# Attention a of a hybrid block: loop of four steps written out, three small jobs moved from VectorE to ScalarE

## The chip, the cores and the metric

One core of one Trainium2 chip runs the whole kernel. The metric is the device time of one execution in microseconds; the median of three runs of the kernel before is 5300.36 us (5296.66 to 5301.02). Engines are named as the profile names them: PE is TensorE's matmuls, PEld its weight loads, DVE VectorE, ACT ScalarE, POOL GpSimd, SP SyncE; a q behind the name is the engine's sequencer, which runs waits, register operations, branches and DMA issues.

## The reference

A block of four sublayers on x of shape (32, 256, 128) in float32: attention a, a mixture of experts, attention b, the mixture of experts again, each on a layer norm of x and added to x. Only attention a is touched by the change:

```python
q, k, v = split_heads(layernorm(x) @ W_qkv.T + b_qkv)      # 16 heads of 8
scores = einsum('bhid,bhjd->bhij', q, k) * 128 ** -0.5     # 256 x 256 per head
topk_scores, indices = top_k(scores, 76)                   # int(256 * 0.3) per row
masked = full(-inf); masked[..., indices] = topk_scores
attn = softmax(masked)
x = x + (attn @ v).reshape(32, 256, 128) @ W_out.T + b_out
```

So each row of 256 scores keeps its 76 largest and loses the rest before the softmax.

## The kernel before

Attention a runs before L1109, the two expert stages and attention b after it; those are not touched. Its work is cut into 64 groups, two for each of the 32 sequences: a group is 8 heads, and a head has 256 x 256 scores, so a group is 16 tiles of 128 rows x 256 scores. Several groups are under way at once, one step apart: in step t PE computes the scores of group t+1, ACT and POOL find thresholds for group t, DVE takes the largest values of group t-1, the rest of group t-2 is judged, and groups t-3 and t-2 go through exponentials and the product with v.

Every engine runs the same list of steps. `schedule` (L423) calls `step(t, b, u)` with t the step, b the sequence and u = t mod 4, which picks the buffers: step -1, steps 0 to 3 as straight code, then an `eng.Fori` of 14 trips with four steps in each (t = 4 to 59), then steps 60 to 67 as straight code. Inside the loop the values that engines wait for are computed from the loop register. Even steps also prepare the next sequence (norm, projections of q and k), odd ones finish that (rows of q, spreads, values). The order inside a step is written out by hand for every engine, and engines meet by semaphores only.

For one group, in the order of the work:

* PE writes the scores of a head into one of three PSUM banks (L644). DVE copies them to SBUF, two tiles a head (`evac`, L950 to L964); the copy (L960) also leaves each row's maximum in `mxs`. After the eighth head L964 writes the negated maxima `nmx`, and SP waits for that (`s["nmx"]`, L540), stores them to DRAM (L544) beside copies of q and k, and reads them back turned into one row of `q4x` for each head (L551). The matching row of k is the constant 1 (`onerow`, L269 and L802), so that the matmul of L671 yields scores less their row's maximum.
* ACT counts, by three passes of Sign with a running sum (L844), how many scores of a row lie above a guess; POOL moves the guess after the first two passes (`move`, L475) and after the third makes `hi_t` and `kk` (L502, L504), for which DVE waits at L1053.
* DVE takes for every tile the 16 largest values not above `hi_t` (`largest`, L966: one pass to zt, then MAX8, MATCH_REPLACE8, MAX8), and between these, piece by piece, `picks` (L991) chooses the 76th largest into `mid` and the one after it into `nxt`, and forms `fail`, 1 for a row whose threshold isn't certain. Two reduces (L1004, L1005) do the choosing.
* PE sums `fail` over the partitions (`judged`, L663, one row of 16 numbers in PSUM bank M1). In the middle of a step DVE turns them into integers (`check_flags`, L1034), reduces them to one (L1036), and its sequencer loads that one into a register and branches (`redo`, L1083): past the repair code when it is 0, which it is in all but two steps. Only then is `s["okay"]` raised (L1038), for which POOL waits before it makes `gone` (L494), the terms that push dropped scores far down.
* PE forms the scores again, less the maximum (L671), adds `gone` (L678), ACT takes exponentials (L830), PE multiplies by v (L692), and the sums, the division (`normalise`, L1019) and the output projection follow.

For the guess of the next sequence DVE also copies the rows of k and q from PSUM to `ktok` and `qtok` (`take_k` L912, `take_qr` L916), at h == 7 of even and h == 3 of odd steps.

Of the kernel before, what the change touches and what calls it, by code (L numbers as in the profile page):

```python
# [4 lines left out]
BATCH, T, D = 32, 256, 128  # L5
P = 128
# [50 lines left out]
def build(nc, x, W_qkv, b_qkv, W_out, b_out, Wq, Wk, Wv, Wp, pos, gate_w, gate_bias,  # L57
# [7 lines left out]
    with ctx:  # L65
# [17 lines left out]
        onerow = sb("onerow", [P, 1])  # L83
# [74 lines left out]
        with nc.Block() as block:  # L158
# [65 lines left out]
            def _(dve):  # L224
# [44 lines left out]
                nc.vector.tensor_reduce(onerow[:, :], ident[:, :].rearrange("p (n w) -> p n w", w=PAD16)[:, :, HD], AX, ALU.add)  # L269
# [42 lines left out]
        def ab(name, shape, dt=f32):  # L312
# [20 lines left out]
        nmx = ab("nmx", [P, NB4, GT])  # L333
# [15 lines left out]
        mid = ab("mid", [P, NB4, GT])  # L349
        fine = ab("fine", [P, NB4, GT])  # L350
        fail = ab("fail", [P, GT])
# [9 lines left out]
                      "nmx copied turned spgate out pused pt pv on own aown pown slow oc gate pgate upper vput ini inid")  # L361
        nmx_rows = nc.dram_tensor("nmx_rows", (P, GT), f32, kind="Internal").ap()
# [58 lines left out]
        BODY = (1, BATCH // 2 - 1)  # L421

        def schedule(eng, step):  # L423

            step(-1, -1, 3)
            for u in range(4):
                step(u, 0, u)
            with eng.Fori(*BODY) as i:
                for u in range(4):
                    step(i * 4 + u, i * 2 + u // 2, u)  # L430
            for i in (BODY[1], BODY[1] + 1):
                for u in range(4):
                    if 4 * i + u <= GROUPS + 3:
                        step(4 * i + u, 2 * i + u // 2, u)

        with nc.Block() as block:
            @block.gpsimd
            def _(pool):
# [31 lines left out]
                def step(t, b, u):  # L470
# [14 lines left out]
                    def outsiders(lag, heads):  # L485
# [3 lines left out]
                        for h in heads:  # L489
                            wait(pool, s["pused"], 8 * (t - lag) + h - 3)  # L490
                            pool.sem_inc(s["pgate"], 1)
                            for i in range(HALVES):
                                c = 2 * h + i
                                last = pool.tensor_scalar(gone[:, h % 4, i, :], SS[:, (u - lag) % 4, c, :], mid[:, (u - lag) % 4, c:c + 1], 0.0,  # L494
                                                          ALU.subtract, ALU.min)
# [35 lines left out]
            def _(sp):  # L531
# [4 lines left out]
                def step(t, b, u):  # L536
# [3 lines left out]
                    wait(sp, s["nmx"], t + 1)  # L540
# [3 lines left out]
                    sp.dma_start(nmx_rows, nmx[:, u, :]).then_inc(s["copied"], 16)  # L544
# [4 lines left out]
                    rows = nmx_rows.rearrange("q (e g i) -> e g i q", e=2, i=HALVES)  # L549
# [9 lines left out]
            def _(pe):  # L559
# [98 lines left out]
                def step(t, b, u):  # L658
# [4 lines left out]
                    def judged():  # L663

                        wait(pe, s["failed"], t - 1)
                        use1(m1_before(bb, "f0" if even else "f1"))
                        nc.tensor.matmul(M1[0:1, 0:GT], ones128[:, :], fail[:, :], start=True, stop=True).then_inc(s["m1"], 1)
# [119 lines left out]
            def _(act):  # L787
# [10 lines left out]
                def take_q(m, b, par, n):  # L798
                    wait(act, s["m0"], n + 1)
                    wait(act, s["copied"], COPIED * 2 * (b - 1))  # L800
                    if m == 2:
                        last = nc.scalar.activation(k4[:, par, :, :].rearrange("p c t -> p (c t)"), M0[:, :], ACT.Identity, bias=onerow[:, 0:1])  # L802
# [13 lines left out]

                take_x(0)
                for m in range(3):
                    take_q(m, 0, 0, m + 1)
                take_qn(4)  # L820
                take_v(0, 7)
# [11 lines left out]
                def step(t, b, u):  # L833
# [18 lines left out]
                    for h in range(9):  # L852
                        if h >= 2 and h % 2 == 0:
                            late, a = PAIRS[h // 2 - 1]
                            exponentials(t - late, a)
                            exponentials(t - late, a + 1)
                        if runs(t):
# [5 lines left out]
                        if even and front:  # L863
                            if h == 2:
                                take_x(m0_before(bb, "xT"))
                            if h in (4, 5, 6):
                                take_q(h - 4, bb + 1, (par + 1) % 2, m0_before(bb, ("q0", "q1", "k")[h - 4]))
                            if h == 8:
                                take_qn(m0_before(bb, "qn"))
                        if not even and h == 4 and runs(bb, 2, BATCH):  # L870
# [13 lines left out]
            def _(dve):  # L884
# [27 lines left out]
                def take_k(n):  # L912
                    wait(dve, s["m1"], n + 1)
                    V.tensor_copy(ktok[:, :, :].rearrange("p i d -> p (i d)"), M1[:, 0:T]).then_inc(s["m1c"], 1)

                def take_qr(n):  # L916
                    wait(dve, s["m0"], n + 1)
                    V.tensor_copy(qtok[:, :, :].rearrange("p i d -> p (i d)"), M0[:, 0:T]).then_inc(s["m0c"], 1)

# [16 lines left out]
                take_k(0)  # L936
                take_qr(5)
# [4 lines left out]
                def step(t, b, u):  # L942
# [7 lines left out]
                    def evac(h):  # L950
# [11 lines left out]
                        if h == 7:  # L962
                            wait(dve, s["evac"], GT * (t + 1) + GT)
                            V.tensor_scalar(nmx[:, (u + 1) % 4, :], mxs[:, (u + 1) % 4, :], -1.0, None, ALU.mult).then_inc(s["nmx"], 1)  # L964
# [26 lines left out]
                    def picks():  # L991
# [12 lines left out]
                        mids = own.mark(V.tensor_reduce(mid[:, z2, :], pick[:, 0, :, :], AX, ALU.add))  # L1004
                        nexts = own.mark(V.tensor_reduce(nxt[:, :], pick[:, 1, :, :], AX, ALU.add))  # L1005
                        yield
                        own.need(nexts)
                        apart = own.mark(V.tensor_tensor(nxt[:, :], nxt[:, :], mid[:, z2, :], ALU.is_lt))
                        yield
                        own.need(apart)  # L1010
                        positive = own.mark(V.scalar_tensor_tensor(tmp[:, :], mid[:, z2, :], 1.0e-6, nxt[:, :], ALU.is_gt, ALU.mult))
# [5 lines left out]
                        V.tensor_scalar(fail[:, :], fine[:, z2, :], -1.0, 1.0, ALU.mult, ALU.add).then_inc(s["failed"], 1)  # L1017
# [25 lines left out]
                    for h in range(8):  # L1043
# [14 lines left out]
                        if front and even and h == 7:  # L1058
# [858 lines left out]
```

## Time and profile before

| what | value |
|---|---|
| median of three runs | 5300.36 us |
| the profiled execution | 5302.46 us |
| its span | 5300.7 us |
| PE busy in the span | 4709.3 us, 89% |
| DVE busy | 4089.0 us, 77% |
| ACT busy | 3157.1 us, 60% |
| POOL busy | 2522.7 us, 48% |
| mean granted clock of TensorE | 0.814 of 2.4 GHz |

The profile is one execution on the chip, and all the rows come from it. Busy time counts compute instructions; waits, register operations and branches are not in it. An average over the span hides that the stages differ: attention a is the part up to about 2560 us, in which DVE is the fullest engine; in the parts after it PE is. In a timeline a row begins with its start in microseconds from the span's start, then its length, engine, line, operation, output and inputs; the bracket is the time that the engine sat idle before it, and what ended that.

### The profile page before, as it was taken

The numbers are of one execution on the slowest core, as the hardware profiler recorded it, in microseconds if no ns is written. First come the engines' busy times: TensorE is split into PE (matmuls) and PEld (weight loads), VectorE is DVE, ScalarE is ACT, GpSimd is POOL, SyncE is SP. The second block draws the span as 40 slices with busy tenths as digits, with TensorE's granted clock in tenths as the row PEclk, the third lists the DMA queues.
The fourth block names the chain that finished last, engine by engine and source line by source line (L and its number), as shares of the span: only waits on it lengthen the run. The fifth ranks groups of instructions, "written<-read, shape, count | busy, mean of one in ns | idle before, by whom it ended". The sixth has DMA issues, their size and how long they took to land. (4 is left out here: it accounts for less than half of the span.)

```text
span 5300.7 us, 121671 instructions
## 1 busy us (share of the span) xinstructions
PE 4709.3 (89%) x34686; PEld 3284.1 (62%) x34686; DVE 4089.0 (77%) x14487; ACT 3157.1 (60%) x10145; POOL 2522.7 (48%) x3026
## 2 busy tenths in 40 slices
PE   4588888889878898898899999899999998999998
PEld 3344444445444454454688888766666666888887
DVE  3899999999989999999588888655555555888886
ACT  3688888888867888887222222376777775222222
POOL 1466666666656666666544444311111111444444
PEclk6566666666656666656899999999999999999999
DMA  2000000000000000000234443200000001444444
GB/s 70 10 14 10 13 10 13 10 13 10 13 10 10 13 10 13 13 10 10 49 81 84 89 84 80 53 10 10 10 10 10 11 11 36 81 80 82 89 85 96
DMA packets 358589, 188.51 MB, mean 36 GB/s; under 512 B 190691, under 2 KB 346886, under 8 KB 358150
## 3 DMA queue, kind: packets, MB, share of 16 engines
q1 hardware_dynamic: 358150, 183.55, 17.3%
q8 instruction: 167, 2.74, 0.2%
q14 instruction: 272, 2.23, 0.1%
HBM read 147.04 MB, written 11.01 MB: 30 GB/s over the span
## 5 line engine op out<-in xcount | busy, mean ns | idle before, releaser
L844 ACT ACTIVATE junk<-SS,nt 128x256 bf16<-128x256 f32 x3072 | 1516.4, 501 | 207.1 <-POOL nt L482 156.5
L494 POOL TENSOR_SCALAR gone<-SS,mid 128x256 bf16<-128x256 f32 x1024 | 1181.9, 1171 | 759.8 <-DVEq L1038 576.5
L1205 POOL TENSOR_TENSOR f_hid<-f_g_m,f_cbs 128x256 f32<-128x256 f32 x1024 | 745.7, 728 | 849.0 <-DVE f_g_m L1450 622.5
L1305 ACT ACTIVATE f_th<-bank 128x256 f32<-128x256 f32 x1088 | 418.5, 385 | 1146.0 <-PE bank L1236 1146.0
L1235 PE MATMUL bank<-f_xTf,wgT 128*128 128x256 f32 x2176 | 692.6, 400 | 52.1 <-DVE f_g_m L1450 36.4
L1851 DVE TENSOR_REDUCE nmxb<-bank 128x2 f32<-128x512 f32 x512 | 329.2, 685 | 476.1 <-PE bank L1623 476.0
L1236 PE MATMUL bank<-f_xTf,wuT 128*128 128x256 f32 x2176 | 651.8, 381 | 0.0
L644 PE MATMUL bank<-k,q 32*128 32x256 f32 x2048 | 452.7, 574 | 220.0 <-DVE SS L960 216.6
L1267 PEld LDWEIGHTS bank<-wdT,f_hid 128*128 128x128 f32 x4096 | 601.0, 191 | 68.0 <-POOL f_hid L1205 13.2
L1267 PE MATMUL bank<-wdT,f_hid 128*128 128x128 f32 x4096 | 629.7, 276 | 11.0 <-POOL f_hid L1205 10.9
L844 ACT ACTIVATION_READ_ACCUMULATOR junk<-SS,nt 128x1 f32 x3072 | 594.0, 193 | 0.0
L975 DVE SCALAR_TENSOR_TENSOR zt<-SS,hi_t 128x256 f32<-128x256 f32 x1024 | 485.5, 514 | 89.2 <-issue 47.5
L671 PE MATMUL bank<-q4x,k4x 32*128 32x256 f32 x2048 | 535.1, 596 | 8.3 <-ACT pT L830 8.3
L1442 DVE SCALAR_TENSOR_TENSOR f_g_s<-f_th,bank 128x256 f32<-128x256 f32 x1088 | 451.3, 415 | 107.1 <-ACT f_th L1305 87.5
L1450 DVE TENSOR_TENSOR f_g_m<-f_g_s,bank 128x256 f32<-128x256 f32 x1088 | 455.9, 419 | 75.2 <-DVE f_g_s L1442 3.5
L1742 ACT ACTIVATE probb<-bank,nmxb 128x256 f32<-128x256 f32 x1024 | 441.6, 496 | 78.3 <-DVE nmxb L1851 78.3
L644 PEld LDWEIGHTS bank<-k,q 32*128 32x128 f32 x2048 | 264.2, 270 | 348.1 <-DVE SS L960 280.7
L1552 POOL TENSOR_TENSOR q<-qrow,mask_h 128x1024 f32<-128x1024 f32 x64 | 137.2, 2145 | 716.9 <-DMA qrow<-q_rows 652.9
L1236 PEld LDWEIGHTS bank<-f_xTf,wuT 128*128 128x128 f32 x2176 | 416.7, 191 | 57.4
L692 PE MATMUL bank<-pT,vaug 128*32 128x256 f32 x2048 | 425.5, 559 | 0.7 <-issue 0.6
L984 DVE MATCH_REPLACE8 zt<-L,zt 128x256 f32<-128x256 f32 x1024 | 409.0, 405 | 0.0
L830 ACT ACTIVATE pT<-bank 128x512 f32<-128x512 f32 x512 | 275.0, 588 | 220.6 <-PE bank L678 220.1
(233 smaller groups left out, 8037.1 us busy)
## 6 DMA issues: line engine op xcount, KB each, us to landing
f_cbs<-f_shares SPq DMA_DIRECT2D x512, 256.0 KB, 5.8
q4x<-q SPq DMA_DIRECT2D x64, 256.0 KB, 2.4
k4x<-k SPq DMA_DIRECT2D x64, 128.0 KB, 2.1
qrow<-q_rows SPq DMA_DIRECT2D x512, 8.0 KB
q_rows<-qTb SPq DMA_DIRECT2D x32, 128.0 KB, 1.7
out_dram<-xres SPq DMA_DIRECT2D x4, 1024.0 KB, 9.3
q4x<-nmx_rows SPq DMA_DIRECT2D x128, 4.0 KB
f_shares<-f_combT SPq DMA_DIRECT2D x64, 32.0 KB, 1.4
```

Of the source, the lines that this page charges most:

```text
L494: last = pool.tensor_scalar(gone[:, h % 4, i, :], SS[:, (u - lag) % 4, c, :], mid[:, (u - lag) % 4, c:c + 1], 0.0, ALU.subtract, ALU.min)
L644: last = nc.tensor.matmul(S[h % 3][:, i * T:(i + 1) * T], q4[rows(h), par, 2 * (u % 2) + h // 4, i * P:(i + 1) * P], k4[rows(h), par, u % ...
L671: nc.tensor.matmul(PT[h % 2][:, k * T:(k + 1) * T], k4x[rows(h), v, k * P:(k + 1) * P], q4x[rows(h), v, h // 4, :], start=True, stop=False)
L844: nc.scalar.activation(junk[:, c % 2, :], SS[:, uu % 4, c, :], ACT.Sign, bias=bias(c), accum_out=acc[:, k, uu % 4, c:c + 1]).then_inc(s["s ...
L975: n = own.mark(V.scalar_tensor_tensor(zt[:, i, :], SS[:, z, c, :], hi_t[:, y, c:c + 1], SS[:, z, c, :], ALU.is_le, ALU.mult))
L1205: pool.tensor_tensor(hid[:, e % NBUF, :], g_m[:, e % NBUF, :], cbs[:, par, e, :], ALU.mult).then_inc(s["hid"], 1)
L1235: nc.tensor.matmul(g[:, 0:T], wgT[:, e, :], xTf[:, par, :], start=True, stop=True)
L1236: nc.tensor.matmul(g[:, T:2 * T], wuT[:, e, :], xTf[:, par, :], start=True, stop=True).then_inc(s["gu"], 1)
L1267: last = nc.tensor.matmul(Y[par][h][:, 0:D], src[:, h * P:(h + 1) * P], wdT[:, e, :], start=(e == 0), stop=(e == NBLK - 1))
L1442: n = own.mark(V.scalar_tensor_tensor(g_s[:, e % 3, :], th[:, e % 3, :], 1.0, g[:, 0:T], ALU.add, ALU.mult))
L1450: V.tensor_tensor(g_m[:, e % NBUF if e < EB else NBUF, :], g_s[:, e % 3, :], g[:, T:2 * T], ALU.mult).then_inc(s["gm"], 1)
L1742: last = nc.scalar.activation(probb[:, u % 4, i, :], S[u % 4][:, i * T:(i + 1) * T], ACT.Exp, bias=nmx[:, u % 4, i:i + 1], scale=1.0)
```

## The change

`schedule` calls `step` for t = -1 and then for t = 0 to 67, all as straight code, and the waits are on constants. Five more edits go with it, all in attention a:

* The maxima are not negated: L964 and `nmx` go, SP waits for the copies' own semaphore and stores `mxs`, and the constant row of k is -1 (`minusrow`) in place of 1.
* `take_k` and `take_qr` are done by ACT, with `nc.scalar.copy`, at h == 7 of even and h == 2 of odd steps.
* The two reduces of `picks` are one reduce that writes both results to `mid`, which has two rows for each buffer.
* `fail` has 17 columns; the last is the sum over the 16, made by the accumulator of the same instruction, and PE sums all 17 over the partitions.
* ACT copies the 17 sums to the integers `flags`, at h == 4 after its exponentials. DVE's cast and its reduce to one number go; DVE waits for ACT's copy, raises the gate semaphore and loads the number.

```diff
@@ -266,7 +266,8 @@
                 nc.vector.tensor_copy(pext[:, mid + 2 * REL:], pext[:, mid + 2 * REL - 1:mid + 2 * REL].to_broadcast([HD, tail])).then_inc(s_pext, 1)
                 dve.wait_ge(s_const, 1)
                 nc.vector.tensor_tensor(mask_h8[:, :], mask_h16[:, 0:HG], mask_h16[:, HG:H], ALU.add)
-                nc.vector.tensor_reduce(onerow[:, :], ident[:, :].rearrange("p (n w) -> p n w", w=PAD16)[:, :, HD], AX, ALU.add)
+                own.link(nc.vector.tensor_reduce(minusrow[:, :], ident[:, :].rearrange("p (n w) -> p n w", w=PAD16)[:, :, HD], AX, ALU.add))
+                nc.vector.tensor_scalar(minusrow[:, :], minusrow[:, :], -1.0, None, ALU.mult)
                 dve.wait_ge(s_trc, (NJ + 3) // 4)
 
         def norm_dve(dve, own, b, s):
@@ -418,20 +418,12 @@
         PAIRS = ((3, 2), (3, 4), (3, 6), (2, 0))
         SUMS = ((3, 0), (3, 2), (3, 4), (3, 6))
 
-        BODY = (1, BATCH // 2 - 1)
 
         def schedule(eng, step):
 
             step(-1, -1, 3)
-            for u in range(4):
-                step(u, 0, u)
-            with eng.Fori(*BODY) as i:
-                for u in range(4):
-                    step(i * 4 + u, i * 2 + u // 2, u)
-            for i in (BODY[1], BODY[1] + 1):
-                for u in range(4):
-                    if 4 * i + u <= GROUPS + 3:
-                        step(4 * i + u, 2 * i + u // 2, u)
+            for t in range(GROUPS + 4):
+                step(t, t // 2, t % 4)
 
         with nc.Block() as block:
             @block.gpsimd
@@ -537,16 +529,16 @@
                     par = u // 2 % 2
                     if not runs(t):
                         return
-                    wait(sp, s["nmx"], t + 1)
+                    wait(sp, s["evac"], GT * t + GT)
                     sp.sem_inc(s["spgate"], 1)
                     wait(sp, s["pused"], 8 * (t - 3))
                     sp.sem_inc(s["spgate"], 1)
-                    sp.dma_start(nmx_rows, nmx[:, u, :]).then_inc(s["copied"], 16)
+                    sp.dma_start(max_rows, mxs[:, u, :]).then_inc(s["copied"], 16)
                     sp.dma_start(q4x[:, u, :, :], q4[:, par, 2 * (u % 2):2 * (u % 2) + 2, :]).then_inc(s["copied"], 16)
                     sp.dma_start(k4x[:, u, :], k4[:, par, u % 2, :]).then_inc(s["copied"], 16)
                     wait(sp, s["copied"], COPIED * (t + 1))
                     sp.sem_inc(s["spgate"], 1)
-                    rows = nmx_rows.rearrange("q (e g i) -> e g i q", e=2, i=HALVES)
+                    rows = max_rows.rearrange("q (e g i) -> e g i q", e=2, i=HALVES)
                     for e in range(2):
                         sp.dma_start(q4x[HD + PAD16 * e:P:PAD32, u, e, :].rearrange("g (i q) -> g i q", i=HALVES), rows[e],
                                      allow_slow_non_contiguous=True).then_inc(s["turned"], 16)
@@ -664,7 +656,7 @@
 
                         wait(pe, s["failed"], t - 1)
                         use1(m1_before(bb, "f0" if even else "f1"))
-                        nc.tensor.matmul(M1[0:1, 0:GT], ones128[:, :], fail[:, :], start=True, stop=True).then_inc(s["m1"], 1)
+                        nc.tensor.matmul(M1[0:1, 0:GT + 1], ones128[:, :], fail[:, :], start=True, stop=True).then_inc(s["m1"], 1)
 
                     def below_max(v, h, k):
 
@@ -814,10 +806,20 @@
                     wait(act, s["m0"], n + 1)
                     nc.scalar.activation(qnat[:, :], M0[:, 0:T], ACT.Identity, bias=bnat[:, 0:1]).then_inc(s["m0c"], 1)
 
+                def take_k(n):
+                    wait(act, s["m1"], n + 1)
+                    nc.scalar.copy(ktok[:, :, :].rearrange("p i d -> p (i d)"), M1[:, 0:T]).then_inc(s["m1c"], 1)
+
+                def take_qr(n):
+                    wait(act, s["m0"], n + 1)
+                    nc.scalar.copy(qtok[:, :, :].rearrange("p i d -> p (i d)"), M0[:, 0:T]).then_inc(s["m0c"], 1)
+
                 take_x(0)
                 for m in range(3):
                     take_q(m, 0, 0, m + 1)
                 take_qn(4)
+                take_k(0)
+                take_qr(5)
                 take_v(0, 7)
                 own.end()
 
@@ -854,6 +856,10 @@
                             late, a = PAIRS[h // 2 - 1]
                             exponentials(t - late, a)
                             exponentials(t - late, a + 1)
+                        if h == 4 and runs(t, 2):
+                            f1 = m1_before(bb, "f0" if even else "f1")
+                            wait(act, s["m1"], f1 + 1)
+                            nc.scalar.copy(flags[:, :], M1[0:1, 0:GT + 1]).then_inc(s["m1c"], 1)
                         if runs(t):
                             k, j = h // 3, h % 3
                             ready, done, bias = PASS[k]
@@ -865,8 +871,12 @@
                                 take_x(m0_before(bb, "xT"))
                             if h in (4, 5, 6):
                                 take_q(h - 4, bb + 1, (par + 1) % 2, m0_before(bb, ("q0", "q1", "k")[h - 4]))
+                            if h == 7:
+                                take_k(m1_before(bb, "ktok"))
                             if h == 8:
                                 take_qn(m0_before(bb, "qn"))
+                        if not even and front and h == 2:
+                            take_qr(m0_before(bb, "qtok"))
                         if not even and h == 4 and runs(bb, 2, BATCH):
                             wait(act, s["m0"], m0_before(bb, "oT") + 1)
                             nc.scalar.copy(oT[:, :], M0[:, 0:T]).then_inc(s["m0c"], 1)
@@ -909,14 +919,6 @@
                         n = V.tensor_scalar(xn[:, h, :], xrow(b, h), mv[:, h, 0:1], rstd[:, h:h + 1], ALU.subtract, ALU.mult)
                     n.then_inc(s["xn"], 1)
 
-                def take_k(n):
-                    wait(dve, s["m1"], n + 1)
-                    V.tensor_copy(ktok[:, :, :].rearrange("p i d -> p (i d)"), M1[:, 0:T]).then_inc(s["m1c"], 1)
-
-                def take_qr(n):
-                    wait(dve, s["m0"], n + 1)
-                    V.tensor_copy(qtok[:, :, :].rearrange("p i d -> p (i d)"), M0[:, 0:T]).then_inc(s["m0c"], 1)
-
                 def take_g(n):
                     wait(dve, s["m1"], n + 1)
                     V.tensor_tensor(gram[:, :], M1[:, 0:P], mask_bd[:, :, :].rearrange("p h d -> p (h d)"), ALU.mult).then_inc(s["m1c"], 1)
@@ -933,8 +935,6 @@
 
                 statistics(0)
                 normed(0)
-                take_k(0)
-                take_qr(5)
                 take_g(1)
                 take_mom(0, 6, 6)
                 own.end()
@@ -959,9 +959,6 @@
                             c = 2 * h + i
                             V.tensor_scalar(SS[:, (u + 1) % 4, c, :], S[h % 3][:, i * T:(i + 1) * T], 1.0, -3.0e38, ALU.mult, ALU.max,
                                             accum_out=mxs[:, (u + 1) % 4, c:c + 1]).then_inc(s["evac"], 1)
-                        if h == 7:
-                            wait(dve, s["evac"], GT * (t + 1) + GT)
-                            V.tensor_scalar(nmx[:, (u + 1) % 4, :], mxs[:, (u + 1) % 4, :], -1.0, None, ALU.mult).then_inc(s["nmx"], 1)
 
                     def largest(lag, p, between):
 
@@ -1001,20 +998,20 @@
                         above = own.mark(V.tensor_tensor(fine[:, z2, :], L[:, y, :, 0], hi_t[:, y, :], ALU.is_lt))
                         yield
                         own.need(second)
-                        mids = own.mark(V.tensor_reduce(mid[:, z2, :], pick[:, 0, :, :], AX, ALU.add))
-                        nexts = own.mark(V.tensor_reduce(nxt[:, :], pick[:, 1, :, :], AX, ALU.add))
+                        both = own.mark(V.tensor_reduce(mid[:, z2, :, :].rearrange("p a t -> p (a t)"),
+                                                        pick[:, :, :, :].rearrange("p a t j -> p (a t) j"), AX, ALU.add))
                         yield
-                        own.need(nexts)
-                        apart = own.mark(V.tensor_tensor(nxt[:, :], nxt[:, :], mid[:, z2, :], ALU.is_lt))
+                        own.need(both)
+                        apart = own.mark(V.tensor_tensor(nxt[:, :], mid[:, z2, 1, :], mid[:, z2, 0, :], ALU.is_lt))
                         yield
                         own.need(apart)
-                        positive = own.mark(V.scalar_tensor_tensor(tmp[:, :], mid[:, z2, :], 1.0e-6, nxt[:, :], ALU.is_gt, ALU.mult))
+                        positive = own.mark(V.scalar_tensor_tensor(tmp[:, :], mid[:, z2, 0, :], 1.0e-6, nxt[:, :], ALU.is_gt, ALU.mult))
                         yield
                         own.need(positive)
                         both = own.mark(V.tensor_tensor(fine[:, z2, :], fine[:, z2, :], tmp[:, :], ALU.mult))
                         yield
                         own.need(both)
-                        V.tensor_scalar(fail[:, :], fine[:, z2, :], -1.0, 1.0, ALU.mult, ALU.add).then_inc(s["failed"], 1)
+                        V.tensor_scalar(fail[:, 0:GT], fine[:, z2, :], 0.0, 0.0, ALU.is_equal, ALU.add, accum_out=fail[:, GT:GT + 1]).then_inc(s["failed"], 1)
 
                     def normalise():
 
@@ -1030,10 +1027,8 @@
 
                     def check_flags():
                         n1 = m1_before(bb, "f0" if even else "f1")
-                        wait(dve, s["m1"], n1 + 1)
-                        V.tensor_copy(flags[:, 0:GT], M1[0:1, 0:GT]).then_inc(s["m1c"], 1)
                         wait(dve, s["m1c"], n1 + 1)
-                        own.link(V.tensor_reduce(flags[:, GT:GT + 1], flags[:, 0:GT], AX, ALU.max))
+                        dve.sem_inc(s["gate"], 1)
                         redo(dve, V, z2)
                         dve.sem_inc(s["okay"], 1)
 
@@ -1055,13 +1050,9 @@
                             normalise()
                         if h == 4 and runs(t, 2):
                             check_flags()
-                        if front and even and h == 7:
-                            take_k(m1_before(bb, "ktok"))
                         if front and not even:
                             if h == 1:
                                 take_g(m1_before(bb, "gram"))
-                            if h == 3:
-                                take_qr(m0_before(bb, "qtok"))
                             if h == 5:
                                 take_mom(bb + 1, m0_before(bb, "mom"), m0_before(bb, "qtok") + 1)
                         if h == 7 and not even and tail:
...
```

## Rows read from the trace of the kernel before

**Rows 1.** Windows, 402 to 1451 us: time, then busy (count) of PE, PEld, DVE, ACT, POOL, clock, DMA.
```profile
402.00:1451.00 1049.00, 927.19 (x4538) 514.21 (x4540) 971.41 (x3782) 857.71 (x3126) 684.22 (x763) 0.64 0.07 12
```

**Rows 2.** Waits of DVE, 60 to 2560 us: line, releaser, total us, times, longest.
```profile
DVE stats L895 <- issue: 51.1, 13, 4.1
DVE zt L975 <- issue: 47.5, 34, 3.1
DVE work L1095 <- issue: 36.1, 2, 19.3
DVE zt L975 <- DVE flags L1036: 28.9, 29, 1.0
...
DVE flags L1034 <- PE bank L667: 3.8, 9, 2.3
```

**Rows 3.** Timeline of DVE, end of the even step t = 24.
```profile
1029.71 0.07 DVE L960 DVE_READ_ACCUMULATOR SS<-bank 128x1 f32 x1
1029.82 0.17 DVE L964 TENSOR_SCALAR nmx<-mxs 128x16 f32<-128x16 f32 x1
1029.92 0.42 DVE L914 COPY ktok<-bank 128x256 f32<-128x256 f32 x1
1030.26 1.11 DVE L975 SCALAR_TENSOR_TENSOR zt<-SS,hi_t 128x256 f32<-128x256 f32 x2
```

**Rows 4.** Timeline of DVE, after the flags in two straight steps past the loop.
```profile
2384.20 1.10 DVE L975 SCALAR_TENSOR_TENSOR zt<-SS,hi_t 128x256 f32<-128x256 f32 x2 [1.31 <-issue]
...
2419.03 1.10 DVE L975 SCALAR_TENSOR_TENSOR zt<-SS,hi_t 128x256 f32<-128x256 f32 x2 [0.99 <-DVE flags L1036]
```

**Rows 5.** Timeline of DVE around the flags, an even and an odd step.
```profile
1017.23 0.16 DVE L1034 CAST flags<-bank 1x16 int32<-1x16 f32 x1
...
1018.58 1.10 DVE L975 SCALAR_TENSOR_TENSOR zt<-SS,hi_t 128x256 f32<-128x256 f32 x2 [1.00 <-DVE flags L1036]
...
1051.91 0.16 DVE L1034 CAST flags<-bank 1x16 int32<-1x16 f32 x1
...
1053.56 1.10 DVE L975 SCALAR_TENSOR_TENSOR zt<-SS,hi_t 128x256 f32<-128x256 f32 x2 [1.30 <-issue]
```

**Rows 6.** Timeline of DVE, the two reduces.
```profile
1003.92 0.40 DVE L1004 TENSOR_REDUCE mid<-pick 128x16 f32<-128x240 f32 x1
1004.24 0.39 DVE L1005 TENSOR_REDUCE nxt<-pick 128x16 f32<-128x240 f32 x1
```

**Rows 7.** Costliest groups of the page, a wider reduce: busy, mean ns, idle before.
```profile
L1851 DVE TENSOR_REDUCE nmxb<-bank 128x2 f32<-128x512 f32 x512 | 329.2, 685 | 476.1 <-PE bank L1623 476.0
```

**Rows 8.** Timeline of PE, flags of an even step, then part of the odd one.
```profile
1014.82 0.21 PE L667 MATMUL bank<-fail,ones 128*1 128x16 f32 x2
...
1043.80 2.08 PE L644 MATMUL bank<-k,q 32*128 32x256 f32 x8 [0.18 <-DVE SS L960]
...
1051.36 0.21 PE L667 MATMUL bank<-fail,ones 128*1 128x16 f32 x2
1052.04 1.22 PE L644 MATMUL bank<-k,q 32*128 32x256 f32 x4 [0.47 <-DVE SS L960]
```

**Rows 9.** Groups of ACT by line, 402 to 1451 us, small copies: busy, mean ns.
```profile
L872 ACT COPY oT<-bank 128x256 f32<-128x256 f32 x14 | 5.0, 357 | 0.0
L795 ACT ACTIVATE xsum<-xsum 128x1 f32<-128x1 f32 x14 | 2.8, 203 | 0.4
```

**Rows 10.** Timeline of ACT, exponentials of the odd step.
```profile
1048.86 1.09 ACT L830 ACTIVATE pT<-bank 128x512 f32<-128x512 f32 x2 [1.54 <-PE bank L678]
...
1058.55 1.09 ACT L830 ACTIVATE pT<-bank 128x512 f32<-128x512 f32 x2 [2.95 <-PE bank L678]
```

**Rows 11.** Timeline of DVE, start of the even step t = 26.
```profile
1070.38 0.42 DVE L960 TENSOR_SCALAR_CACHE_REDUCE SS<-bank 128x256 f32<-128x256 f32 x1 [0.23 <-PE bank L644]
...
1076.99 0.88 DVE L975 SCALAR_TENSOR_TENSOR zt<-SS,hi_t 128x256 f32<-128x256 f32 x2
```

**Rows 12.** Timeline of POOL, start of the even step t = 26.
```profile
1076.59 0.20 POOL L504 TENSOR_SCALAR kk<-acc 128x16 f32<-128x16 f32 x1
```

More of the change, by code:

```diff
@@ L82, in build @@
         bqs = sb("bqs", [P, 2, 2])
-        onerow = sb("onerow", [P, 1])
+        minusrow = sb("minusrow", [P, 1])
         wvT = sb("wvT", [P, D])
@@ L332, in build @@
         mxs = ab("mxs", [P, NB4, GT])
-        nmx = ab("nmx", [P, NB4, GT])
         acc = ab("acc", [P, 3, NB4, GT])
@@ L348, in build @@
         nxt = ab("nxt", [P, GT])
-        mid = ab("mid", [P, NB4, GT])
+        mid = ab("mid", [P, NB4, 2, GT])
         fine = ab("fine", [P, NB4, GT])
-        fail = ab("fail", [P, GT])
+        fail = ab("fail", [P, GT + 1])
         flags = ab("flags", [1, GT + 1], mybir.dt.int32)
@@ L360, in build @@
         s = sems("a", "mv rstd xn m0 m0c m1 m1c var sig scores evac signs u0 u1 u2 thr failed flag okay "
-                      "nmx copied turned spgate out pused pt pv on own aown pown slow oc gate pgate upper vput ini inid")
-        nmx_rows = nc.dram_tensor("nmx_rows", (P, GT), f32, kind="Internal").ap()
+                      "copied turned spgate out pused pt pv on own aown pown slow oc gate pgate upper vput ini inid")
+        max_rows = nc.dram_tensor("max_rows", (P, GT), f32, kind="Internal").ap()
         COPIED, TURNED = 48, 32
@@ L493, in outsiders @@
                                 c = 2 * h + i
-                                last = pool.tensor_scalar(gone[:, h % 4, i, :], SS[:, (u - lag) % 4, c, :], mid[:, (u - lag) % 4, c:c + 1], 0.0,
+                                last = pool.tensor_scalar(gone[:, h % 4, i, :], SS[:, (u - lag) % 4, c, :], mid[:, (u - lag) % 4, 0, c:c + 1], 0.0,
                                                           ALU.subtract, ALU.min)
@@ L801, in take_q @@
                     if m == 2:
-                        last = nc.scalar.activation(k4[:, par, :, :].rearrange("p c t -> p (c t)"), M0[:, :], ACT.Identity, bias=onerow[:, 0:1])
+                        last = nc.scalar.activation(k4[:, par, :, :].rearrange("p c t -> p (c t)"), M0[:, :], ACT.Identity, bias=minusrow[:, 0:1])
                     else:
@@ L1086, in redo @@
                     slow = Own(dve, s["slow"])
-                    any_failed = dve.value_load(flags[0:1, GT:GT + 1], min_val=0, max_val=P)
+                    any_failed = dve.value_load(flags[0:1, GT:GT + 1], min_val=0, max_val=P * GT)
                     with dve.If(any_failed > 0):
@@ L1102, in redo @@
                                 slow.link(V.tensor_tensor(src, src, w, ALU.add))
-                                low = mid[:, z, bass.ds(c, 1)]
+                                low = mid[:, z, 0, bass.ds(c, 1)]
                                 slow.link(V.tensor_scalar(low, low, 0.0, -0.5 * FAR, ALU.mult, ALU.add))
```

## The prediction

> **What bounds the kernel now.** I read the busy time by windows first, then DVE's waits, then the timelines of one loop trip on each engine. Only the stage of attention a changes, some 2500 of the 5300.7 us. In its middle [rows 1] DVE is busy 971 of 1049 us, PE 927, ACT 858, POOL 684, and PE's granted clock averages 0.64 (mostly 1.2 GHz, the rest 2.4 GHz). Three engines are near full, so the order of the waits decides. DVE's waits over the whole stage [rows 2] are nearly all its own: 51.1 us in front of L895, 13 times, which is the jump back of the loop (14 trips, 13 jumps); 47.5 + 28.9 us in front of L975, mostly the fetch of the flags; 36.1 us in the repair path, taken in two steps. For the flags it waits on PE 9 times and 3.8 us. So DVE sets the pace, and each microsecond taken off it shortens a step until another engine is late. From start to start of L964 [one of them in rows 3] an ordinary step takes 36.2 to 36.4 us, one with a jump back 40.2, four of them 148.5.
>
> **The change part by part, on DVE's path.** There are 64 steps, 32 pairs of an even and an odd one.
>
> *Loop written out.* The jump costs 51.1 / 13 = 3.9 us [rows 2]; step against step it is 40.2 - 36.4 = 3.8. Thirteen of them: -50. PE, ACT, POOL and SP jump too, beside it. What may come in its place is the fetching of long straight code. The last steps of the kernel before are straight code already, and the two stops there that hold a skip over the repair code last 1.31 and 0.99 us [rows 4], as inside the loop: 1.30 and 1.00 [rows 5]. I cost the fetch at 0; its other end is a rival below.
> The Trainium skill (Runtime: NRT & Kernel Launch, section Instruction fetch mechanics) says that a taken branch whose target isn't in the small window of code already fetched stalls until it is. By that rule the jump of 3.9 us goes, which the sum has already; a skip that leaves the window would cost as much, which none of these rows shows.
>
> *Maxima not negated.* The last accumulator read starts at 1029.71, ktok's copy at 1029.92 [rows 3]: L964 costs 0.21 us, x 64 = -13. The sign moves into a constant row of k. SP stores mxs where it stored nmx, the same DMAs and bytes, 0.2 us earlier.
>
> *Rows copied by ScalarE.* ktok's copy holds DVE from 1029.92 to 1030.26 [rows 3] = 0.34 us, and qtok's, of the same shape, as long. Each is in 31 pairs: -21.
>
> *Two reduces made one, an accumulator added.* Now 0.32 us from start to start and 0.39 for the second = 0.71 [rows 6]. A reduce over 512 elements takes 0.685 [rows 7], and 480 some 0.64 to 0.69: -0.02 to -0.07 a step. The fail instruction gets an accumulator read, 0 to +0.08 by those in [rows 3]. Together -4 to +4 us; I take -2.
>
> *Flags fetched by ScalarE.* In an even step the cast starts at 1017.23 and work resumes at 1018.58 [rows 5]: 1.35 us. Cast and reduce are 0.39 of it; in the other 0.96 DVE's sequencer loads the flag into a register, checks it, skips the repair code and raises a semaphore, with DVE empty. Afterwards cast and reduce are gone: -0.39 at least. The load then waits for ACT's copy and no longer for DVE's own reduce, so it can run ahead beside the two score copies in front (0.7 us). No row shows a register load beside a busy DVE: this part is worth 0 to 0.7. I take the nearest cover, less some 0.15 for the order of issue: 0.39 + 0.55 = 0.9 us for an even step. Over all 64 steps -25 to -58.
> That needs the flags early. In the even step PE sums them at 1014.82, 2.4 us before the cast [rows 8, 5]. In the odd step L667 starts at 1051.36 and ends 0.3 us before the cast of 1051.91 [rows 8, 5], and in about half of the odd steps the cast follows it at once (9 of these show as waits [rows 2]). There ACT's copy (0.20 us for 128x1 to 0.36 for 128x256 [rows 9]) takes the cast's place, the register load follows it, and nothing is gained.
>
> Sum if nothing else were late: 50 + 13 + 21 + 2 + 58 = 144 us.
>
> **What is late next.**
> (a) *PE in the odd steps.* From the scores at 1043.80 PE works without a break to the flags at 1051.36 and waited only 0.18 and 0.47 us for DVE [rows 8]; at 1070.38 DVE itself waits 0.23 us for PE [rows 11]. So between 1043.8 and 1070.4 DVE can gain some 0.47 us at 1.2 GHz, where the edits save 0.34 + 0.9 + 0.21 = 1.45. That holds for about half of the 32 odd steps (in the others PE had 2.4 GHz for a while and was 1 to 2 us ahead): 16 x 1.0 = +16.
> (b) *POOL after an odd step.* It works without a break from DVE's release to 1076.59 + 0.20 [rows 12], and DVE, which needs its result, goes on at 1076.99 [rows 11]. DVE can be there 0.1 us earlier, of 0.28 saved on the way: about +4.
> (c) *PE before the first score copy of an odd step.* By my reading of those copies against L644 it has 0.3 to 0.7 us of room in a quarter of the cases and about 2 in the rest, against 1.5 saved: 8 x 1.0 = +8.
> (d) *The jump.* Its 3.8 us gave PE and POOL time to catch up; half a microsecond of each comes back: 13 x 0.3 = +4.
> Together +32, so **-112 us**, 1 us a step beside the jumps.
>
> *ACT* gets (0.36 + 0.36) / 2 + 0.2 = 0.56 us a step. It is busy 858 / 1049 = 82% of a mean step of 37.1 us [rows 1], 30.3, then 30.9 of 35.4, 87%. In odd steps it will stand behind L667: its exponentials of 1048.86 end at 1049.95 and L667 at 1051.57, 1.6 us. But it stands 2.95 us before those of 1058.55 [rows 10], which hides both. Cost 0; without that cover 1.6 + 0.56 in an odd step. The prologue, the last steps (which wait on PE) and the two repairs stay.
>
> **The time.** The sum is made against the profiled execution, 5302.46 us, and gives 5190; the median of the runs is 2.1 below it: 5188. Some of what a denser PE wins back by its clock is likelier than nothing, 2 us of term (a): I forecast **5186 us**.
>
> **Rivals.**
> 1. *The sequencer gains nothing, or ACT is in the way* (chance 0.14). If the register load still finds DVE empty, 0.5 x 32 = 16 us go; if ACT's stand behind L667 delays its sums, another 0.6 x 32 = 19: 5186 + 16 to 35 = 5202 to 5221. For it: no row of a load beside work. Against: the idle 2.95 us of ACT.
> 2. *The straight code brings waits of its own* (0.05). The loop goes, but a third of the 64 skips leave the fetched code. The longest stop in front of L975 is 3.1 us [rows 2] against 1.3: 20 x 1.8 = +36, and with like stops on ACT or PE about 50: 5236. Against: [rows 4].
> 3. *Slower* (0.04). The same at every skip and at the jump's price: 64 x 3.9 = 250 us against 112, 5300 + 138 = 5438; it is slower as soon as 29 of the 64 skips leave the fetched code. For it: each trip pays such a jump now. Against: none of the skips in the straight steps does. It is the skill's rule above turned against this change.
> 4. *PE follows* (0.09). A denser PE is granted 2.4 GHz more often, term (a) goes, and in odd steps the flags are early: 5186 - 16 - 14 = 5156, and 5300 - 144 - 5 = 5151 at most.
>
> **How the numbers follow.** The forecast has 0.67 (its own range 5168 to 5205), the rivals what stands with them, and 0.01 is left for an effect within 0.2% (10.6 us, about what a measurement of this kernel can tell from none). The range goes down to rival 4 and up past rival 1: 5150 to 5224. Faster 0.95, same 0.01, slower 0.04.
>
> **What would show it.** DVE has no wait of 3.9 us in front of L895; after the fetch of the flags it stops 0.4 to 0.5 us in even steps and about 1 us in odd ones, released by PE's L667 or ACT's copy. Four steps take 139 to 143 us. PE's waits for L960 shrink to some 0.1 us in odd steps, and DVE waits for L644 in more places than now. ACT waits 1 to 2 us for L667 in odd steps and less before L830. The forecast is wrong if four steps take over 145 us, if stops of 3 us or more stand behind the skips, or if DVE waits for ACT's work rather than PE's or POOL's.

## The result and the profile after

The changed kernel takes 5290.01 us (median of 13 runs, 5268.32 to 5301.59) against 5301.02 for the kernel before: ratio 0.9975, 95% interval 0.9964 to 0.9986. It is 11 us faster where 115 were forecast. The forecast sign was right, the size wrong by a factor of ten, and the time lies outside the range of 5150 to 5224. The profiled execution is the slowest of the 13, 5301.59 us, so its profile shows a kernel as long as the one before. One execution of the kernel before took 15943 us and one of the first experiment 8362 us; the ratios leave both out.

The middle of the stage, columns as in [rows 1]:

```profile
402.00:1451.00 1049.00, 928.03 (x4546) 510.97 (x4543) 951.35 (x3674) 866.81 (x3191) 692.32 (x765) 0.64 0.07 12
```

DVE is relieved, 951 us against 971, and PE is as busy as before, 928 us against 927, at the same granted clock of 0.64. The waits of DVE over 60 to 2560 us, which answer to [rows 2]:

```profile
DVE SS L960 <- PE bank L636: 134.3, 58, 8.3
DVE zt L972 <- issue: 62.6, 59, 3.1
DVE work L1086 <- issue: 38.4, 2, 19.6
```

The jumps' 51.1 us are gone, the stops behind the flags take 62.6 us where they took 76.4, and all of it has come back as waits for the first scores of a step (L636), 134.3 us where the whole stage had 26.5. Measured from the last L960 of a step to that of the next, averaged over t = 7 to 37, a step took 40.2, 36.3, 36.3, 36.0 us in a trip of the loop (148.8) and takes 37.1, 37.1, 37.2, 37.2 now (148.5). So what the jump took in one step is now lost in small parts in all four. What PE waits for, 330 to 1480 us (31 steps), the kernel before and then the changed one:

```profile
PE bank L644 <- DVE SS L960: 96.8, 62, 6.2
PE bank L575 <- DVE xn L909: 28.3, 16, 5.3
PE bank L702 <- DVE gram L922: 8.6, 5, 2.1
PE bank L583 <- ACT q L805: 4.6, 8, 0.8
PE bank L619 <- ACT oT L872: 0.2, 1, 0.2
```

```profile
PE bank L636 <- DVE SS L960: 31.8, 19, 3.0
PE bank L694 <- DVE gram L924: 26.0, 15, 1.9
PE bank L575 <- ACT q L797: 22.9, 16, 1.6
PE bank L611 <- ACT oT L882: 22.6, 15, 2.3
PE bank L567 <- DVE xn L919: 19.6, 16, 5.2
```

The two lines of the first list that name ACT are 4.8 us together, and 45.5 in the second: 16 times 1.4 us in even steps for the copy of q, 15 times 1.5 in odd ones for that of oT. PE also waits 26.0 us for DVE's `gram` where it waited 8.6, but it does so in the fastest kernel of all too (25.7). Here is where the waits for ACT come from, first PE, then ACT, in one odd step:

```profile
1044.89 0.22 PE L659 MATMUL bank<-fail,ones 128*1 128x17 f32 x2
1045.20 2.07 PE L636 MATMUL bank<-k,q 32*128 32x256 f32 x8
1048.66 1.20 PE L611 MATMUL bank<-gram,qnat 128*128 128x128 f32 x4 [1.38 <-ACT oT L882]
```

```profile
1045.14 0.16 ACT L862 CAST flags<-bank 1x17 int32<-1x17 f32 x1 [1.24 <-PE bank L659]
1045.21 0.50 ACT L846 ACTIVATE junk<-SS,nt 128x256 bf16<-128x256 f32 x1
...
1048.17 0.34 ACT L882 COPY oT<-bank 128x256 f32<-128x256 f32 x1
```

ACT stands (sits idle in a wait) 1.24 us before the flags, then counts six tiles, and only then copies oT, which PE's spreads (L611) wait for. In the kernel before no such stand was there, and the copy of oT was over at 1053.14, 0.9 us before PE came to its spreads (L619):

```profile
1052.78 0.36 ACT L872 COPY oT<-bank 128x256 f32<-128x256 f32 x1
...
1054.04 1.22 PE L619 MATMUL bank<-gram,qnat 128*128 128x128 f32 x4
```

In an even step it is the same with q, and here the record of PE's sum of the flags misleads:

```profile
1081.36 0.64 PE L684 MATMUL bank<-pT,vaug 128*32 128x256 f32 x2
1081.38 0.21 PE L659 MATMUL bank<-fail,ones 128*1 128x17 f32 x2
1081.78 1.49 PE L684 MATMUL bank<-pT,vaug 128*32 128x256 f32 x6
1083.21 1.50 PE L575 MATMUL bank<-xT,wqsT 128*128 128x256 f32 x4
...
1087.25 1.96 PE L575 MATMUL bank<-xT,wqsT 128*128 128x256 f32 x4 [1.48 <-ACT q L797]
```

```profile
1083.37 0.16 ACT L862 CAST flags<-bank 1x17 int32<-1x17 f32 x1 [1.03 <-remote]
```

The sum is recorded at 1081.38, but ACT gets its flags at 1083.37, just after the matmuls of the weighing (L684, the product with v), issued ahead of the sum, have ended at 1083.27. The semaphore that the sum raises tells the same in the trace: it rises at 1083.35, 1.75 us after the record has ended, and as the profile finds no record that ended then, it calls the releaser `remote`. The kernel before has the same distance of 1.75 us in 30 of its 32 even steps. In all odd steps but one, where two transposes (L701, L709 before) stand between the weighing and the sum, it is 0.01. Both ends of the ring of waits then show on DVE. The register load did run ahead in even steps: it is recorded from 1083.66 to 1083.97, while DVE copies scores until 1084.08, and DVE stops 0.51 us where [rows 5] had 1.00 behind the cast and reduce. And a step's first score copy waits 2.30 us for PE.

```profile
1064.96 0.43 DVE L960 TENSOR_SCALAR_CACHE_REDUCE SS<-bank 128x256 f32<-128x256 f32 x1 [2.30 <-PE bank L636]
...
1084.60 1.10 DVE L972 SCALAR_TENSOR_TENSOR zt<-SS,hi_t 128x256 f32<-128x256 f32 x2 [0.51 <-issue]
```

### The profile page after: what moved, and what is told of

It reads as the page before. It is cut to its first block and busy times, and to the rows that moved or that the text cites. A ratio compares the mean times of both kernels' runs of the same rounds, so it can differ in the third digit from the quotient of the medians.

```text
span 5299.8 us, 115583 instructions
## 1 busy us (share of the span) xinstructions
PE 4712.4 (89%) x34686; PEld 3276.2 (62%) x34686; DVE 4037.9 (76%) x14232; ACT 3170.0 (60%) x10273; POOL 2533.6 (48%) x3026
## 5 line engine op out<-in xcount | busy, mean ns | idle before, releaser
L486 POOL TENSOR_SCALAR gone<-SS,mid 128x256 bf16<-128x256 f32 x1024 | 1204.0, 1191 | 645.4 <-DVEq L1033 465.8
L972 DVE SCALAR_TENSOR_TENSOR zt<-SS,hi_t 128x256 f32<-128x256 f32 x1024 | 484.5, 514 | 85.7 <-issue 62.6
L636 PE MATMUL bank<-k,q 32*128 32x256 f32 x2048 | 430.6, 555 | 104.5 <-DVE SS L960 99.6
L960 DVE TENSOR_SCALAR_CACHE_REDUCE SS<-bank 128x256 f32<-128x256 f32 x1024 | 385.0, 413 | 134.3 <-PE bank L636 134.3
L684 PE MATMUL bank<-pT,vaug 128*32 128x256 f32 x2048 | 429.8, 565 | 10.9 <-issue 10.8
L1226 PEld LDWEIGHTS bank<-f_xTf,wgT 128*128 128x128 f32 x2176 | 331.5, 192 | 119.5 <-DVE f_g_m L1441 107.4
```

Of the source, the lines that this page charges most:

```text
L636: last = nc.tensor.matmul(S[h % 3][:, i * T:(i + 1) * T], q4[rows(h), par, 2 * (u % 2) + h // 4, i * P:(i + 1) * P], k4[rows(h), par, u % ...
L972: n = own.mark(V.scalar_tensor_tensor(zt[:, i, :], SS[:, z, c, :], hi_t[:, y, c:c + 1], SS[:, z, c, :], ALU.is_le, ALU.mult))
L1226: nc.tensor.matmul(g[:, 0:T], wgT[:, e, :], xTf[:, par, :], start=True, stop=True)
```

## The experiments

Theory A1: ACT's stand before the flags delays its copies of q and oT, and a ring of waits runs through these, PE's next scores and DVE's first score copy. Theory A2: PE's own work at the granted clock is a floor of 148 us for four steps. Times of four steps are measured as above. Each result is a median; the ratio is to the kernel before on the same chip, with its 95% interval.

**Loop written out, nothing else.**

```diff
-            with eng.Fori(*BODY) as i:
...
+            for t in range(GROUPS + 4):
+                step(t, t // 2, t % 4)
```

> The kernel before with the loop written out and nothing else. Theory A (a ring of waits through PE is nearly as tight as DVE's own pace, and the 3.9 us pause at each jump was time in which PE and POOL caught up): most of the 50 us of jumps is given back as waits of DVE for the first scores of a step, 5 to 25 us faster than before. Theory B (the jumps are a plain loss of DVE, and the loss sits in the other edits): 40 to 50 us faster than before, about 5255.

5254.57 us, ratio 0.9907 (0.9892 to 0.9922). Theory B was right on this term: 47 us, the jumps' -50 of the sum. Four steps take 144.8 us, and apart from two stops of 3.1 us behind the repairs, which the kernel before has too, DVE's longest stop behind a skip is 1.34 us (1.33 before). PE's work is the same here, at a granted clock of 0.65, so A2's floor of 148 us isn't one.

**The changed kernel with the loop kept.**

```diff
-            for t in range(GROUPS + 4):
-                step(t, t // 2, t % 4)
+            with eng.Fori(*BODY) as i:
...
```

> The changed kernel with the loop of four steps put back, all other edits kept. Theory A: DVE has slack in every step now, so the jumps fall into it: within 15 us of the changed kernel, about 5290 to 5305. Theory B: the jumps cost 50 us again: 5340.

5267.29 us, 0.9932 (0.9919 to 0.9946): faster than the changed kernel by 23 us. Neither theory had that. Writing out the loop is worth 47 us alone and does harm beside the late flags. With the loop the step with the jump takes 38.5 us and the three behind it 37.0, 35.7 and 35.2 instead of 37.1 to 37.2. PE's waits for q fall from 22.9 to 12.3 us, those for oT only from 22.6 to 20.2.

**Flags copied by DVE again, the other edits kept.**

```diff
-                            wait(act, s["m1"], f1 + 1)
-                            nc.scalar.copy(flags[:, :], M1[0:1, 0:GT + 1]).then_inc(s["m1c"], 1)
...
+                        wait(dve, s["m1"], n1 + 1)
+                        V.tensor_copy(flags[:, :], M1[0:1, 0:GT + 1]).then_inc(s["m1c"], 1)
```

> The changed kernel with the 17 flags copied by DVE again (the second reduce stays out). Theory A1 (the stand of ACT behind PE's sum of flags delays its next copies, of q in even and of oT in odd steps, and PE's ring of waits runs through these: 1.4 us each): PE's waits for ACT's q and oT, 45 us in 31 steps in the changed kernel, nearly go, and the kernel is 25 to 70 us faster than the changed one, 5220 to 5265. Theory A2 (PE's own work at the granted clock is the floor, whoever copies the flags): within 10 us of the changed one, or slower by the 0.5 to 0.9 us a step that DVE gets back, up to +50.

5225.84 us, 0.9862 (0.9847 to 0.9877), 64 us faster than the changed kernel. PE's waits for ACT:

```profile
PE bank L575 <- ACT q L797: 4.4, 9, 0.8
...
PE bank L611 <- ACT oT L878: 1.6, 2, 0.8
```

A1, and not A2. With the first experiment it splits the change: loop -47; the maxima, the reduce and the row copies together -29, in which DVE's reduce of the flags (L1036) is counted, since it stays out here; the copy of the flags on ACT +64.

**Another order on ACT: two counts, oT, flags, the other counts.**

```diff
+                            if h == 4:
+                                count(t, k, u, bias, ready, done, range(first, first + 2))
+                                take_o()
+                                take_flags()
+                                first += 2
```

> The changed kernel with another order on ACT only: in the middle of a step ACT counts two tiles before it takes oT and then the flags, and counts the rest after. Same instructions, same work. Theory A1: ACT no longer stands idle 1.0 to 1.2 us before the flags, q and oT are copied 1 to 2.5 us earlier, and PE's waits for them go: 40 to 90 us faster than the changed kernel, 5200 to 5250. Theory A2: within 10 us of the changed kernel.

5212.82 us, 0.9826 (0.981 to 0.9843): 77 us for an order, with all the instructions of the change. PE's list no longer has a wait for oT, that for q is 6.8 us, and the granted clock between 402 and 1451 us is 0.68 where it was 0.64.

**Only oT's copy moved ahead of the flags.**

```diff
-                        if not even and h == 4 and runs(bb, 2, BATCH):
...
+                        if not even and h == 4 and runs(bb, 2, BATCH):
+                            wait(act, s["m0"], m0_before(bb, "oT") + 1)
+                            nc.scalar.copy(oT[:, :], M0[:, 0:T]).then_inc(s["m0c"], 1)
                         if h == 4 and runs(t, 2):
```

> The changed kernel with one copy moved: in odd steps ACT copies oT ahead of its wait for the flags, not five counts after it. ACT's stand before the flags (1.0 to 1.2 us) stays. If the ring through PE is what counts, PE's wait for oT (22.6 us in 31 steps) goes, 32 odd steps x 1.4 = 45 us faster at most, 5245 to 5265; the wait for q in even steps stays. If the idle of ACT before the flags is what counts (its whole load), no more than 10 us faster.

5230.52 us, 0.9872 (0.9857 to 0.9887): 60 us, more than its wait and more than the range had. ACT still stands 18.1 us before oT (16 times) and 8.2 before the flags, 26.3 together where the changed kernel had 34.5 before the flags. Most of ACT's idle stays and most of the loss goes, so it is the late copy that costs. PE's wait for q, which was expected to stay, halves, 22.9 to 11.0 us; why isn't shown.

**PE's sum of the flags issued ahead of the weighing.**

```diff
+                        if d == 1 and runs(t, 2):
+                            judged()
                         late, a = SUMS[d]
                         weigh(t - late, (u - late) % 4, a)
...
-                            if runs(t, 2):
-                                judged()
```

> The changed kernel with PE's sum of the flags issued ahead of the eight matmuls of the weighing in front of it and not behind them, nothing else. The trace shows that matmul's record some 1.3 us before ACT is released in even steps; if the release really comes only when the matmuls ahead of it are through, moving it makes the flags 1.0 to 1.9 us earlier in both kinds of step, ACT has no stand before them, and q and oT are in time: 60 to 90 us faster than the changed kernel, 5200 to 5230, as with the other order on ACT (5213). If ACT waited for something else in even steps, only the odd ones gain: 30 to 45, about 5250.

5201.13 us, 0.9815 (0.9801 to 0.9828), 89 us faster than the changed kernel and 101 faster than the one before: the best version. In odd steps the sum now also stands ahead of the two transposes of oT (L701). Between 330 and 1480 us ACT has no wait for the flags left, PE waits 6.3 us for q and 3.6 for oT, and the sum's semaphore rises 0.01 us after its record ends in all 64 steps. So the release in even steps had come late because of the matmuls ahead of it.

**The new order on ACT, with the loop.**

```diff
-            for t in range(GROUPS + 4):
+            with eng.Fori(*BODY) as i:
...
```

> The kernel with the new order on ACT (5213 us) with the loop of four steps put back. If the written-out loop is worth its 13 jumps once nothing else is late: 5213 + 35 to 50 = 5248 to 5263. If it's worth nothing or does harm, as beside the late flags (5290 with straight code, 5267 with the loop): 5190 to 5215.

5250.63 us, 0.9905 (0.989 to 0.992): straight code is worth 38 us again once q and oT are in time.

**Rows of k and q copied by DVE again, late flags kept.**

```diff
+                        if front and even and h == 7:
+                            take_k(m1_before(bb, "ktok"))
...
+                            if h == 3:
+                                take_qr(m0_before(bb, "qtok"))
```

> The changed kernel with the rows of k and q copied by DVE again. If ACT's load is part of what makes q and oT late, taking 0.36 us a step off it gives 5 to 25 us, 5265 to 5285; if it isn't, and DVE has slack here (it waits 2 to 2.8 us for PE at the start of most steps), the time stays within 5 us of 5290; by my first sum DVE would lose 21 us: 5311.

5262.98 us, 0.9923 (0.9909 to 0.9936): 27 us faster, slightly more than expected. Beside late flags the row copies harm when ACT makes them: without them PE's waits for q and oT are 34.9 us and not 45.5.

**Early sum of the flags and oT first.**

```diff
+                        if d == 1 and runs(t, 2):
+                            judged()
...
+                            nc.scalar.copy(oT[:, :], M0[:, 0:T]).then_inc(s["m0c"], 1)
                         if h == 4 and runs(t, 2):
```

> PE's sum of the flags ahead of the weighing (5201 us) and ACT's copy of oT ahead of the flags, together. Theory A1: PE's last waits for oT (3.6 us in 31 steps) go: 0 to 10 us faster than 5201. If the early sum has already taken all that the order of ACT can give, 5196 to 5206. A rival: oT is then waited for by ACT itself, since PE turns it after the sum of flags, and ACT's counts come later: 5205 to 5215.

5214.12 us (5197.75 to 5215.59), 0.9825 (0.9812 to 0.9839). The time is in the rival's range and its wait is there, ACT standing before oT. That it is slower than 5201 isn't shown: the interval overlaps the one there (0.9801 to 0.9828).

```profile
ACT oT L861 <- PE bank L701: 20.6, 16, 1.6
```

**Early sum and row copies on DVE.** The edits are those of the two experiments that made them alone.

```diff
+                        if d == 1 and runs(t, 2):
+                            judged()
...
+                            take_k(m1_before(bb, "ktok"))
```

> PE's sum of the flags ahead of the weighing (5201 us), with the rows of k and q copied by DVE as before the change. Beside late flags these copies on DVE were 27 us faster. If that was because ACT's path was the late one there, it should be gone where ACT has no stand: DVE loses its 0.34 us a step and ACT gains nothing, 5201 + 0 to 20. If the copies on ACT are bad by themselves (a later release of the banks for PE), again 15 to 27 us faster, 5175 to 5186.

5213.39 us, 0.9839 (0.9825 to 0.9852). Where ACT is in time the same copies on DVE cost 12 us instead of giving 27. The 12 is the less certain of the two, for its interval just meets that of 5201 us; a gain of 15 to 27 is ruled out.

**The kernel before with the early sum.**

```diff
+                        if d == 1 and runs(t, 2):
+                            judged()
```

> The kernel before with PE's sum of the flags ahead of the weighing, nothing else. There DVE itself waits for the flags, by the profile only 3.8 us in the whole stage, so the theory that early flags matter only because ACT stands before them says 0 to 10 us faster than before, 5290 to 5302. If early flags are worth 89 us by themselves (whoever fetches them), some 5215 to 5260.

5300.64 us, 0.9998 (0.9989 to 1.0008). Early flags are worth nothing where DVE fetches them and sets the pace.

**Straight code and the flags on ACT, no other edit.**

```diff
-                        V.tensor_copy(flags[:, 0:GT], M1[0:1, 0:GT]).then_inc(s["m1c"], 1)
...
+                            nc.scalar.copy(flags[:, :], M1[0:1, 0:GT + 1]).then_inc(s["m1c"], 1)
```

> The kernel before with the loop written out (5255 us) and the flags fetched by ACT at the place of the change, and no other edit. DVE gains 0.4 to 0.9 us a step by that. Theory A1: ACT's stand delays q and oT and PE waits for them: 10 to 50 us slower than 5255 in spite of it, 5265 to 5305, with 15 to 45 us of PE waits for ACT's q and oT in 31 steps (3.6 without). If the loss needed the other edits too (the copies on ACT above all), 5215 to 5255.

5277.82 us, 0.9956 (0.9942 to 0.9969): 23 us slower than 5255, though DVE has less to do. PE's waits:

```profile
PE bank L612 <- ACT oT L869: 20.2, 15, 2.0
PE bank L576 <- ACT q L798: 19.2, 15, 1.6
```

So the flags on ACT do it by themselves. The 23 us are net of all that DVE saves by it, its reduce included; beside the other edits the copy alone costs 64. That they raise the price because they make DVE faster and ACT fuller fits the experiment with the row copies, but was not taken apart further.

## Why the prediction was wrong

* *What bounds the kernel*: right. DVE set the pace, PE was close behind.
* *The jumps, -50*: right, 47 measured alone, 38 beside timely copies. *Maxima, reduce and row copies*, -36 before what is late next: 29 measured together, DVE's reduce of the flags with them.
* *The flags on DVE's side, 0.9 us in an even step*: about right in size: from the start of the last score copy to the next zt pass took 1.69 us and takes 0.95, 0.74 less. The register load does run beside the score copies. (I split the 1.35 into 0.39 and 0.96; the row has 1.00 of idle.) But I had PE's sum over in even steps 2.4 us before the cast, by the record of L667 in [rows 8]. The weighing in front of it ended only 0.5 us before the cast of 1017.23, and that is when the flags are there:

```profile
1015.22 1.49 PE L692 MATMUL bank<-pT,vaug 128*32 128x256 f32 x6
```

* *"Cost 0 by that cover"* is the step that failed. I saw that ACT would stand 1.6 us behind L667 in odd steps and looked for the cover in its next exponentials (2.95 us idle, [rows 10]) and in POOL. The next work of ACT on which somebody waits is not those but the copy of oT, six counts after the flags, and in even steps that of q. Neither had room: oT's copy was over 0.9 us before PE came to its spreads, and the stand is 1.2 us with the flags' own copy behind it; for q PE waited already, 8 times and 4.6 us. I listed what waits for ACT's sums and not what is queued behind the waiting instruction. The flags term was -58 in the first sum. Alone beside straight code it measured +23, and beside the other edits its copy on ACT measured +64. My own sign of being wrong, four steps over 145 us, is there with 148.5.
* *PE late in odd steps, (a)*: right in place and too small. I let PE cap DVE's gain at 0.47 us, but a PE delayed by 1.4 us in its own unbroken stretch passes most of that on to the step: 45.5 us of waits in 31 steps would be 94 in 64, and the cures gave 60 to 89. Theory A1 is shown by five kernels (the third to the sixth experiment above against the changed kernel, and the last against the first), each moving only the flags or oT.
* *Rival 1* had the mechanism, ACT's stand, and priced it at 35 us at most, by the way through POOL. Rivals 2 and 3 (fetching of straight code) did not occur. Rival 4 can't be separated: most of the faster versions show a higher granted clock (0.65 to 0.68 between 402 and 1451 us, where before and after have 0.64), but the fastest, 5201 us, has 0.66 and not the highest, and none was made to test cause and effect.
* With the two delays away, 5201 us, the forecast is 15 us short: DVE still waits 44.5 us in 31 steps for PE's first scores, more than the 32 us that I had for all that is late next in 64. That kernel has an edit that the forecast didn't, so that the two are so near is in part luck.

Open: why the loop is better than straight code beside the late flags (5267 against 5290). PE's waits for q are rarer with the loop (10 times, not 16); that the pause at the jump lets ACT catch up is a reading of this, not tested. Also open is how much of the 60 us of moving oT alone is clock (0.67 against 0.64).

## What to carry to other kernels

Before a wait is put on another engine, list what that engine has queued behind it up to the next thing that a third engine waits for, and take the room from there: a 0.16 us copy with a 1.2 us stand in front cost 64 us. When a step's engines wait for each other in a ring, work taken off the fullest one shows only if nothing else in the ring grows. The best cure here was to issue the producer earlier (two matmuls moved ahead of eight), 89 us, against 64 for moving the copy back. Judge such edits together as well as alone: the row copies on ACT were worth +27 or -12 us, writing out the loop -47 or +23, by whether one other wait was late.

## What the runs showed of the hardware

* A register load from SBUF runs beside a busy DVE (1083.66 to 1083.97, score copies until 1084.08): the stop in front of L972 is 0.51 us where the same sequence behind cast and reduce took 1.0 to 1.3. In the odd steps, where the flags come when the score copies are over, it isn't shorter (1.53 us at 1046.67).
* A small matmul's record can end 1.75 us before its semaphore rises (1081.60 and 1083.35), when longer ones issued ahead of it are recorded until 1083.27. With the same matmul issued ahead of them it is 0.01 us. The end of such a record isn't the time at which a waiter may go.
* Sixty-four steps of straight code, with nothing else changed, brought DVE no stop of a new kind: two of 3.1 us behind the repairs, as before, and none over 1.34 us in front of that line else.
* The changed kernel's runs spread over 33 us, the faster ones at a higher granted clock (5268.32 at 0.824, 5301.59 at 0.815); which of the two causes the other isn't shown. The kernel before, paced by DVE, has its 12 other runs within 9 us.
